# A four-sequence decoder on one core: a SiLU that reads its bank, and attention rows scaled on ScalarE

## The reference, cut to what matters

```python
# layer 0, block 1, on x (4, 512, 512)
proj = rmsnorm(x, input_ln_w) @ w_in.T
u, gate = split(proj, 2)
u = silu(causal_conv1d(u, conv_w, conv_b))      # four taps, 1024 channels
t_r, Bm, Cm = split(u @ w_x.T, [R, R + N])      # R = 128, N = 16, each rms-normed
dt = softplus(t_r @ w_dt.T + b_dt)
y = selective_scan(u, -exp(A_log), Bm, Cm, D_skip, dt) * silu(gate)
hidden = residual + y @ w_out.T                 # and a feed-forward of width 1408
# layer 0: a second state-space block on ctx (512 channels), a mixture of 8 experts
# layer 1: segmented attention, then
query = ctx @ Wq.T + bq
key = ctx @ Wk.T + bk
attention = softmax(query @ key.T, axis=-1)     # (512, 512) for each sequence
x_m = x @ attention
# and a routed bias
```

## Time and profile before

| | before |
|---|---|
| runs, us | 3115.70, 3117.69, 3120.54 (median 3117.69) |
| profiled execution, us | 3119.29, span 3117.5 |
| PE busy | 2547.0 us (82%), 6708 matmuls |
| DVE busy | 2407.6 us (77%) |
| ACT busy | 1242.0 us (40%) |
| POOL busy | 1052.8 us (34%) |
| mean granted PE clock | 0.881 |
| chain that ended last | PE 41%, DVE 31%, issue 12%, ACT 8%, POOL 4%, DMA 3% |

### The profile page before, as it was taken

The page is one execution under the profiler, slowest core; times in us unless marked ns, Lnnn a source line. Parts: engine busy times, 40 slices in busy tenths (PEclk is TensorE's granted clock), DMA queues, the critical chain, the costliest instruction groups (busy, mean ns, idle before and its releaser), DMA issues.

```text
span 3117.5 us, 21149 instructions
## 1 busy us (share of the span) xinstructions
PE 2547.0 (82%) x6708; PEld 1211.8 (39%) x6708; DVE 2407.6 (77%) x1788; ACT 1242.0 (40%) x1993; POOL 1052.8 (34%) x299
## 2 busy tenths in 40 slices
PE   4787989888969887799698776896987869979965
PEld 1234434333434443344344433443443434445532
DVE  5997898988979988899899989898999883121122
ACT  4334456444353452543534534535335332021231
POOL 1233343344434445424334464244443540000000
PEclk7776999888989998789889997898889879989986
DMA  3124426332212674031126650221266502217810
GB/s 131 29 73 166 137 103 193 103 106 95 64 37 87 216 234 139 26 107 58 38 94 209 220 153 22 94 65 41 75 215 194 155 7 88 71 67 239 284 40 14
DMA packets 160392, 350.13 MB, mean 112 GB/s; under 512 B 30681, under 2 KB 48089, under 8 KB 155609
## 3 DMA queue, kind: packets, MB, share of 16 engines
q1 hardware_dynamic: 134680, 271.89, 28.3%
q10 hardware_dynamic: 20480, 60.10, 5.1%
q0 software_dynamic: 5120, 16.78, 1.6%
HBM read 304.55 MB, written 61.73 MB: 117 GB/s over the span
## 4 chain that ended last, share of the span: by engine, by line
PE 41%; DVE 31%; issue 12%; ACT 8%; POOL 4%; DMA 3%; ACTq 0%; DVEq 0%; SPq 0%; POOLq 0%
DVE hb L1611 13%; PE ps L961 6%; PE ps L968 6%; DVE hb L1619 4%; DVE hb L1524 4%; PE ps L816 4%; PE ps L769 3%; POOL ya L1884 3%; PE ps L823 2%; PE ps L934 2%; PE ps L1004 2%; DMA ring<-in_w_edn 2%; PE ps L1116 2%; PE ps L891 1%; ACT T L1410 1%
## 5 line engine op out<-in xcount | busy, mean ns | idle before, releaser
L1884 POOL TENSOR_TENSOR ya<-ya,hb 128x2048 f32<-128x2048 f32 x188 | 856.7, 4557 | 1334.2 <-DVE hb L1611 1251.1
L1611 DVE TENSOR_TENSOR_SCAN hb<-da,hb 128x2048 f32<-128x2048 f32 x192 | 856.3, 4460 | 2.0 <-ACT da L1158 0.7
L1158 ACT ACTIVATE da<-dl,pk 128x511 f32<-128x511 f32 x768 | 489.3, 711 | 401.1 <-DVE hb L1611 391.0
L1524 DVE TENSOR_TENSOR hb<-du,ps 128x2048 f32<-128x2048 f32 x192 | 436.1, 2271 | 33.8 <-POOL ya L1884 26.1
L1619 DVE TENSOR_TENSOR hb<-hb,ps 128x2048 f32<-128x2048 f32 x192 | 437.6, 2279 | 3.7 <-PE ps L908 2.9
L816 PE MATMUL ps<-V,ring 128*128 128x512 f32 x512 | 245.4, 633 | 20.9 <-DVE V L1552 12.0
L769 PE MATMUL ps<-ring,hid 128*128 128x512 f32 x544 | 247.4, 611 | 3.7 <-DVE hid L1656 3.7
L985 PE MATMUL ps<-ring,hid 128*128 128x352 f32 x480 | 198.1, 496 | 22.2 <-ACT hid L1381 16.2
L989 PE MATMUL ps<-ring,hid 128*128 128x352 f32 x480 | 193.6, 486 | 11.6 <-ACT X L1398 11.5
L1004 PE MATMUL ps<-ring,X 128*128 128x512 f32 x360 | 180.7, 637 | 15.3 <-DMA ring<-in_w_edn 14.5
L961 PE MATMUL ps<-T,ring 128*128 128x512 f32 x352 | 168.7, 624 | 17.5 <-DVE T L1644 17.5
(11 more groups left out here) (283 smaller groups left out, 3457.4 us busy)
## 6 DMA issues: line engine op xcount, KB each, us to landing
ring<-egu SPq DMA_DIRECT2D x240, 352.0 KB, 3.9
ring<-in_w_edn SPq DMA_DIRECT2D x72, 512.0 KB, 5.2
ring<-in_w_fgu SPq DMA_DIRECT2D x44, 512.0 KB, 3.6
hid<-xrows SPq DMA_DIRECT2D x60, 256.0 KB, 4.2
yrows<-X ACTq DMA_DIRECT2D x60, 256.0 KB, 4.7
ring<-wc SPq DMA_DIRECT2D x24, 512.0 KB, 4.3
ring<-in_w_egu SPq DMA_DIRECT2D x24, 512.0 KB, 3.5
ring<-in_w_edn SPq DMA_DIRECT2D x60, 192.0 KB, 4.4
```

The source lines that it names most:

```text
L1158: i = act.activation(dav(n % 2)[:, k, 1:], dl[:, k, 1:], ACT.Exp, scale=Aneg[:, (4 * (u % 3 - 1) if u % 3 else UC) + k, m:m + 1])
L1524: dve.tensor_tensor(hbv(m % NHB), du[:, :, :], wide(ps[:, 5, :], 4), ALU.mult).then_inc(s["dbu"], 1)
L1611: dve.tensor_tensor_scan(hb[:, h, :], da[:, b % 2, :], hb[:, h, :], 0.0, ALU.mult, ALU.add)\
L1884: pool.tensor_tensor(sums, ya[:, :, :], hbv(m % NHB), ALU.add).then_inc(s["acc"], 1)
```

## The change

For sequences 1 to 3, ACT no longer writes `v`. It takes the tangent of the bank plus bias into `ht`, waits for its own write (new semaphore `h_tanh`), and adds one in place (Identity with bias 1.0). DVE then forms `(bank + conv_bA) * ht` in one instruction, straight from PSUM, into `hid`. The bank is now free only when DVE has done that, so the `p_mm` of chunk `n + 4` waits for `h_u` (DVE) where it waited for `h_th` (ACT); the plan's dependency follows. The new DVE line is L1567 of the changed kernel.

In the attention, DVE keeps the reciprocal, and ACT multiplies the row block in place (Copy with a scale from `esum`, L1438 of the changed kernel). The task `att_end` is split: `att_rec` (DVE 0.15, ACT 0.75 in the plan) and `att_end` (PE, ACT).

```diff
         # plan()
-        return ((("p_th", b, m), "act"),) if b else ((("p_ev", b, m), "dve"),)
+        return ((("p_th", b, m), "dve"),) if b else ((("p_ev", b, m), "dve"),)
-                chain(20, ("p_th", b, n), [("act", 1.25), ("dve", 0.7)], (("p_cv", b, n), "pe"),
+                chain(20, ("p_th", b, n), [("act", 1.35), ("dve", 0.7)], (("p_cv", b, n), "pe"),
-            row = chain(60, ("att_end", b, n), [("dve", 0.9), ("pe", 1.0), ("act", 0.6)], row)
+            row = chain(60, ("att_rec", b, n), [("dve", 0.15), ("act", 0.75)], row)
+            row = chain(60, ("att_end", b, n), [("pe", 0.8), ("act", 0.6)], row)
         # PE, p_mm (the same edit at the two places where b > 0 waits)
-                            pe.wait_ge(*of("h_th" if b else "h_conv", b, n - banks(b) + 1))
+                            pe.wait_ge(*of("h_u" if b else "h_conv", b, n - banks(b) + 1))
         # ACT, p_th
                         if b:
-                            act.activation(ucb(b)[:, n, :], ps[:, bank(b, n), :], ACT.Identity, bias=c("conv_bA", n))
                             act.activation(ht[:, n % 2, :], ps[:, bank(b, n), :], ACT.Tanh, bias=c("conv_bA", n))\
+                                .then_inc(s["h_tanh"], 1)
+                            act.wait_ge(s["h_tanh"], UC * (b - 1) + n + 1)
+                            act.activation(ht[:, n % 2, :], ht[:, n % 2, :], ACT.Identity, bias=1.0)\
                                 .then_inc(s["h_th"], 1)
         # ACT, attention
+                    elif t == "att_rec":
+                        act.wait_ge(*of("en_rec", b, n + 1))
+                        act.activation(erow, erow, ACT.Copy, scale=esum[:, n:n + 1]).then_inc(s["en_sc"], 1)
         # DVE, p_th
-                        silu("h", b, n, ht[:, n % 2, :], ucb(b)[:, n, :])
+                        if b:
+                            dve.wait_ge(*of("h_th", b, n + 1))
+                            dve.scalar_tensor_tensor(out=ucb(b)[:, n, :], in0=ps[:, bank(b, n), :], scalar=c("conv_bA", n),
+                                                     in1=ht[:, n % 2, :], op0=ALU.add, op1=ALU.mult).then_inc(s["h_u"], 1)
+                        else:
+                            silu("h", b, n, ht[:, n % 2, :], ucb(b)[:, n, :])
         # DVE, attention
-                    elif t == "att_end":
+                    elif t == "att_rec":
                         dve.wait_ge(*of("en_exp", b, n + 1))
                         dve.reciprocal(esum[:, n:n + 1], esum[:, n:n + 1]).then_inc(s["en_rec"], 1)
-                        dve.wait_ge(*of("en_rec", b, n + 1))
-                        dve.tensor_scalar(erow, erow, esum[:, n:n + 1], None, ALU.mult).then_inc(s["en_sc"], 1)
```

More of the change, by code:

```diff
@@ L402 @@
     [f"slot{i}" for i in range(NSLOT)] + ["pk_in", "eb_in", "memz", "pm_in", "aneg", "set"] +
-    ["u_out0", "u_out1", "z_out0", "z_out1", "t_out", "u_in", "z_in", "t_in", "diag", "wc",
+    ["u_out0", "u_out1", "z_out0", "z_out1", "t_out", "u_in", "z_in", "t_in", "diag", "wc", "h_tanh",
      "c_mm", "c_up", "c_conv", "c_u", "c_th", "c_tr", "c_tn", "c_bc", "h_zt"] +
@@ L808, in _ @@
                         elif n >= UC:
-                            pe.wait_ge(*of("h_th", b, n - banks(b) + 1))
+                            pe.wait_ge(*of("h_u", b, n - banks(b) + 1))
                         elif b > 1:
```

## The result

| | before | changed kernel |
|---|---|---|
| runs, us | 3111.17 to 3123.06, median 3117.69 (13 runs) | 3118.65 to 3134.11, median 3126.33 (13 runs) |
| ratio to before | | 1.0031, 95% interval 1.0020 to 1.0043 |
| profiled execution, us | 3119.29, span 3117.5 | 3130.77, span 3129.0 |
| mean granted PE clock | 0.881 | 0.875 |

The account below looks back on a forecast made before the run. Scans on DVE were taken to set the pace from 700 to 2560 us, PE nearer its limit in the projections; -28 + 0.2 - 13 + 4 + 6 = -30.8 gave 3087 us against the median, 8 in 10 for 3066 to 3106.

Parts of the forecast that it names:

- One more scan step ahead of `ln 2 3`: Step of 8.9 us of DVE, inserted ahead of sequence 3's projections, partly filling idle time: +4 us, bounds 0 and +8.9.
- the scans set the pace there: Between 700 and 2560 us, DVE busy 91% and PE 81%; DVE time ahead of 2543 counts as time.
- Other work that meets POOL: `seg_s`, `comb`, `route_b` and `route_c` shift into or out of stalls beside POOL's sums: +6 us, bounds -4 and +12.
- Attention rows leave DVE: DVE's row scaling, L1762, leaves DVE ahead of 2543 us: -28 us, bounds -19 and -28.
- The activation reads its bank: In the projections, 24 DVE instructions drop to 0.73 us each; 12.8 us on the chain of waits: -13, bounds 0 and -29.7.
- the bank free later: `p_mm` of chunk n + 4 waits for DVE's activation, with 12.5 us of room: 0 us.
- ACT's Copy: Twelve attention Copies ahead of 2543 us, 0.71 us each on ACT, beside DVE's scans: 0 us, bounds 0 and +8.5.
- C: Rival: twelve attention Copies wait on ACT and hold exponentials back, 26 us; 3113 us, no change that counts; chance 0.05.
- E: Rival: the new activation is held beside POOL like L1515, so no early gain; 3100 us; chance 0.05.
- D: Rival: PE waits at `p_mm` for banks that DVE's activation frees late, +53 us; 3140 us, slower; chance 0.05.
- B: Rival: all DVE time freed in attention and projections is time, step filled in, -56 us; 3062 us; chance 0.12.
- A: Rival: PE takes the projections' gain, only attention counts, the step costs 8.9, -13 us; 3105 us; chance 0.17.

Follow-up runs that it names:

- experiment 7: Both edits in the order of the kernel before, with scan step 190 moved ahead of `ln 2 3` on DVE alone: 3096.11 us, ratio 0.9943.
- experiment 1: Both edits, every engine keeping the order of the kernel before: 3084.13 us, ratio 0.9896 to the kernel before.
- experiment 11: Repeat of experiment 1 on another chip, both edits in the order of the kernel before: 3081.26 us, ratio 0.9891.
- experiment 8: Both edits in the order of the kernel before, with scan step 90 moved ahead of `comb` of sequence 0 on DVE alone: 3085.94 us, ratio 0.9916.
- experiment 12: Experiment 1 with four scan steps moved on DVE alone, ahead of `comb` of sequences 0, 1, 2 and `ln 2 3`: 3115.53 us, ratio 1.0001.
- experiment 4: Only the attention rows scaled by ScalarE, early projections and order as in the kernel before: 3097.38 us, ratio 0.9941.
- experiment 3: Only the activation of the early projections reads its bank, attention and order as in the kernel before: 3109.87 us, ratio 0.9973.
- experiment 6: Both edits, ordered by a plan with the split attention entry but the old entries for `p_th`: 3115.02 us, ratio 0.9997 to the kernel before.
- experiment 2: The instructions of the kernel before in the order of the changed kernel: 3148.42 us, ratio 1.0100 to the kernel before.

## Why the prediction was wrong

**The step that failed** is the term "One more scan step ahead of `ln 2 3`", +4 with bounds 0 and +8.9, and under it the premise "the scans set the pace there". It was priced as DVE time that new idle time could fill. Alone it costs 8.6 us in the timeline and 12 in the medians (experiment 7). The steps that the same order puts ahead of `comb` of all three sequences were not priced as steps at all; the prediction priced `comb` and `seg_s` under "Other work that meets POOL", at +6. For both terms together I had +10, at most +21; the order costs 31 us with the old instructions and 43 with the new (1.0031 less 0.9893, the mean of experiments 1 and 11, times 3117). Four steps alone reproduce 33 of these.

Why: between 700 and 2560 us it is the chain of each sequence (`mix`, norms, experts, `comb`, `seg_s`, `xmix`, and the next `mix`) that sets the end. The scans are the work that fills DVE beside it. DVE was 91% busy, but one queue serves both, and a filler step in front of a link delays the link by about the step: 8.8 and 8.9 us at `comb` 0 in experiments 8 and 12, 8.6 at `xmix` 2 in experiment 7. Where the step is missing behind the link a part is given back (5.5 of 8.8 us were left at the next `xmix` in experiment 8); over four steps the total still came to their whole length. Scans done early bought nothing in the changed kernel: there the scan of step 92 starts 13.0 us earlier than before, that of step 144 0.9 us later and the last, 191, 1.5 us earlier, while `xmix` of sequence 2 is 9 us late. The chain in the earlier trace rows passed from `ln 2 3` to `xmix` without a scan, and that was the sign: I read from it where DVE time ends, not what else stood in front of it.

**Attention rows leave DVE**, -28: -20 measured by the medians, -18 by the ratio (experiment 4). The term was mis-sized; the lower bound, the stalls of the five long ones in sequences 1 and 2 at -19, was the better value.

**The activation reads its bank**, -13: -8 measured (experiment 3). In single profiled executions the projections end 10 (experiment 1) to 18 us (experiment 3) earlier, so -13 is possible there, with a part lost later. The sum of 12.8 also took whole durations for instructions that stand on the chain of waits with less: 2.90, 2.90, 0.04 and 4.05 us. Above 0.68 each, that is 7.8, close to what was measured; one chain of one execution does not make that more than a sign. The durations, 0.72 to 0.75 us, were right. PE full at 60.00 of 60 us fits as the place where the rest of the 29.7 went.

**Together** the edits were to bring -41 and bring -32 and -34 by the ratios (1 and 11). The order was to cost +10 and costs +43 with them. So the forecast of -31 became +10 by the ratio: 33 us of the miss are the order, 8 the edits. Of the 43, the attention's entry makes 31 to 32 (experiment 6). The rest, some 11, is open: the entries of `p_th` alone gave 5, not clear of noise, and what the two make together was not tested. The same 12 us show in the table of experiment 2, where the edits bring 33 us in the old order and 21 in the new. DVE's idle time does not explain them: between 700 and 2560 us experiment 11 idles 194 us, as much as the changed kernel's 192, and is ahead by 46 us at `xmix` 2. The two differ in what PE got done, 1540.20 against 1500.89 us:

```profile
700.00:2560.00 1860.00, 1540.20 (x4222) 749.75 (x4221) 1666.19 (x1170) 813.10 (x1330) 784.28 (x211) 0.89 0.35 111
```

**The terms priced at nothing** held: the bank free later (no `p_mm` waits for DVE's activation) and ACT's Copy (3.0 us of waits). ACT's part in the projections shows no new wait; it was not timed alone. Rivals C and E are refuted by the rows of the changed kernel above, D by the banks, for which no `p_mm` waited, B by experiments 1 and 11, where all of DVE's gain without the new order is worth 32 to 34 us and not 56. A was right in two things, a full PE in the projections and a step at its whole 8.9 us, and like the forecast counted one step.

**Other work that meets POOL.** This term was right, and small against the steps. In the profiled execution `seg_s` of sequences 0 and 1 took 2.1 and 2.7 us more (+2.0 each forecast), `comb` of both 0.9 and 1.9 more (+1.4 each), `route_b` of sequence 2 lost its 4.2 and `route_c` gained 3.4 (+3.5): +6.9 where +6 was forecast. The prediction's sentence that a DVE instruction with all tensors in SBUF does not finish before POOL's sum is too wide, though: the reciprocal L1760 at 1192.92, inside the sum of the earlier trace rows, took 0.155 us, and a `tensor_reduce` (L1772 at 2524.38) its 0.686.

**The chances.** Forecast, A, B and E add up to 0.90; less a tenth that is 0.80 or 0.81, not the 0.87 given for "faster".

**What would have shown it**: `ln 2 3` at 2512 was forecast. In experiments 1 and 11, the edits without the order, its statistics start at 2511.59 and 2506.59: the forecast fitted the edits, and the order was what it had missed.

## What to carry over

In a kernel whose engines follow one fixed order, time an edit in the old order first, and the new order with the old instructions second: here the edits were worth -1.1% and the order +1.0% to +1.4%, and together they looked like an edit that does nothing. Count, for each link of the longest dependent chain, how many filler instructions the queue puts in front of it before and after, and price each one more at its whole length until a run says less: four cost 33 us of their 36 here, one alone 6 to 15. The engine's busy share (91% here) does not say that the filler is what counts. Changing an assumed duration in a plan changes the order too, even when the new value is closer to the truth.

## What the runs showed of the hardware

A 128x2048 scan can be held by POOL as well. Of 192 scans before, none took over 4.699 us; in the changed kernel three did, 5.03, 5.29 and 7.35. The timeline of the longest:

```profile
739.05 4.55 POOL L1853 TENSOR_TENSOR X<-X,V 128x2048 f32<-128x2048 f32 x1
740.53 7.35 DVE L1622 TENSOR_TENSOR_SCAN hb<-da,hb 128x2048 f32<-128x2048 f32 x1
```

The same pair before, where the scan starts 0.17 us ahead of POOL's addition:

```profile
741.88 4.42 DVE L1611 TENSOR_TENSOR_SCAN hb<-da,hb 128x2048 f32<-128x2048 f32 x1
742.05 8.59 POOL L1844 TENSOR_TENSOR X<-X,V 128x2048 f32<-128x2048 f32 x1 [0.95 <-DVE V L1638]
```

There the scan takes its 4.42 us and POOL's addition 8.59 in place of 4.55: now POOL is held, for about the length of the scan. The Trainium skill (SBUF — State Buffer, "Who interferes with whom") says that the engine which starts first keeps the other out; this pair of rows agrees. The row at 2406.32, 0.04 us ahead of POOL and held all the same, does not. The traces of all fourteen kernels narrow it down. In them 127 instructions of DVE that read SBUF alone (scans, `scalar_tensor_tensor` and `tensor_scalar`) start up to 0.4 us ahead of a 128x2048 addition of POOL. The 16 with a lead of 0.004 to 0.044 us were all held, by 4.3 to 4.4 us; the 111 with a lead of 0.159 us and more were not. The two groups are not only different forms: L1644, `T<-V,pk,R`, took 5.05 us at 750.59 before, 0.02 us ahead of POOL, and the same instruction 0.72 us at 747.80 in the changed kernel (L1655), 0.21 us ahead. No row has a lead between 0.044 and 0.159.

The granted PE clock moves a product by 2.5 us. The 32 matmuls of the last `xmix` (stretch, busy us, clock, DMA share, GB/s), before:

```profile
3047.20:3061.20 14.00, 13.96 (x32) 1.00 0.00 0
```

and in the changed kernel:

```profile
3054.40:3070.90 16.50, 16.49 (x32) 0.84 0.00 0
```

Over all four `xmix` one matmul takes 592 ns in the median of both kernels, and the longest 697 before and 1193 in the changed kernel, about twice the median: the engine went down to the lower of its two levels, 1.2 GHz, for some of them. In the 13 us ahead of it PE was busy 9.48 of 13.2 us at a granted 0.83 before, and 10.09 of 13.4 at 0.75 in the changed kernel. So 2.5 of the 11.5 us between the two profiled executions are clock. And one execution of a kernel is not its median: with the new activation and the same order up to there, `mix` of sequence 0 came between 688.0 (experiment 3) and 696.6 us (experiment 6).
